# The last key tile of the second product in one stacked pass, ten odd rows in the correction, and x1's changed rows through DRAM

## The chip, the core and the metric
The kernel runs on one core of a Trainium2 chip. The metric is the device time of one execution in microseconds: before the change 171.88 us, the median of 3 runs (171.23 to 172.01). TensorE (PE) does matmuls, VectorE (DVE) elementwise work and reductions, ScalarE (ACT) scaling and roots, GpSimd (POOL) the gathers, SyncE (SP) most of the DMAs.

## The reference
Two graph layers over 1354 nodes of 512 features. The first is an attention over edges; the second a product with the adjacency and a weight.

```python
def layernorm(x): m, v = mean(x), var(x); return (x - m) / sqrt(v + 1e-5)

def L0(x, adj, pairs, Wq, bq, Wk, bk):          # 10000 pairs, 8 heads of 64
    sub, obj = pairs[:, 0], pairs[:, 1]
    att = sum over a head of (x[sub] @ Wq.T + bq) * (x[obj] @ Wk.T + bk) / 8
    scores = zeros(8, n, n);  scores[:, sub, obj] = att
    scores[no edge in adj] = -inf;  scores[diagonal] = 1e-7
    return softmax(scores, axis=2).sum(heads) / 8 @ x

x1  = layernorm(x + L0(x, adj, ...))
out = layernorm(x1 + adj @ (x1 @ W1) + b1)
```

## The kernel before
Nearly all scores are the same constant, since few of the given pairs are edges of the adjacency. So x1 is computed first for every row as if there were none (`sum_neighbours`, L1246: adjacency times x), and the rows with a real pair, at most 64 slots, are computed apart and put in as a correction. A count of pairs that doesn't fit sends every engine into a general path behind a branch (`overflow`, L270); with these inputs it isn't taken. Numbers are held as two f16 halves, high and low, so a product takes two or three matmuls.

Rows are in 11 tiles of 128, the last of 74. x1's tiles become ready one by one: ScalarE writes `x_sb` (L691) and the high half `x1s` (L694), VectorE the low half (L907). Then comes the first product of the second layer, x1 transposed times the adjacency (`mix_rows`, L1303 to L1316): 12 units (4 feature blocks by column spans of 512, 512 and 330), each accumulated over the 11 key tiles in two matmuls, one a half. `MIX_ORDER` sets their order: the first two units go side by side over all key tiles as x1 arrives, then unit by unit; the numbers in `mix_rows(a, b)` are positions in it. Each finished unit is split again into halves (`mix_high` on ScalarE, `mix_low` on VectorE).

Between pieces of that product TensorE does the small matmuls of the slots, in an order written out by hand: flags and numbering of the found pairs (L1320), transposes of gathered rows, queries and keys (L1352), scores (L1369), shares (L1375), the transposed change of x1 (L1380), and its product with W1 (L1387). GpSimd finds the candidates (L606, L611) and gathers x's rows, the sums and the adjacency's columns of the slots (L616 to L636); VectorE does the small steps between. `q` holds a slot's true row of x1, `kk` the row as first computed, `dx1` their difference where the slot counts (`rep`).

In the output stage each tile is 12 matmuls of the product's halves with W1's (`weigh`, L1397) and two of the correction (`correct`, L1421). The correction's stationary side `stackL` has 128 rows: 0 to 62 hold the slots' adjacency columns, 63 ones for the bias, 64 to 127 a one where a slot's row is the output row itself. Its moving side `stackR` holds in the same rows the change times W1, the bias, and `dx1`, as a high and a low half, hence two matmuls. VectorE adds `x_sb` (L1191) and takes moments, ScalarE normalises, SP stores. Six banks rotate (`OUTS`). SP's queue issues its DMAs in program order and stands still at a wait.

Of the kernel before, what the change touches and what calls it, by code (L numbers as in the profile page):

```python
# [34 lines left out]
BIAS_ROW = SLOTS - 1  # L35
SPANS = [(0, 512), (512, 1024), (1024, N)]
# [19 lines left out]
def resnorm_graph(nc, x, adj, pairs, pairs_left, b_qk, w1, b1, adj_t, adj_cols, wq_t, wk_t, adj_diag, out):  # L56
# [5 lines left out]
    with ExitStack() as ctx:  # L62
# [8 lines left out]
        sums_dram = nc.dram_tensor("sums_dram", [NP, GW], f32, kind="Internal").ap()  # L71
        live_map = nc.dram_tensor("live_map", [N, N], f32, kind="Internal").ap()
# [11 lines left out]
        col_rows = flat_stage[0:BIAS_ROW, KF * H:KF * H + N]  # L84
# [21 lines left out]
        stackR = sb("stackR", [P, 2, H], f16)  # L106
# [85 lines left out]
        dT = onehot[:, 0:2 * KF * SLOTS].rearrange("p (a n) -> p a n", a=2)  # L192
# [193 lines left out]
        def general_dve(dve):  # L386
# [186 lines left out]
        def _(pool):  # L573
# [49 lines left out]
            for b in range(YS):  # L623
# [8 lines left out]
                in_offset=bass.IndirectOffsetOnAxis(ap=slot_i[0:BIAS_ROW, 0:1], axis=0)).then_inc(cols_in, 16)  # L632
# [3 lines left out]
            nc.gpsimd.tensor_copy(stackL[0:BIAS_ROW, 0:N], col_rows).then_inc(cols_laid, 1)  # L636
            pool.wait_ge(cols_laid, 1)
# [5 lines left out]
        def _(act):  # L643
# [68 lines left out]
            nc.scalar.activation(stackL[0:64, :], col_no[0:64, :], ACT.Identity, bias=ones[0:64, 0:1], scale=0.0).then_inc(ones_laid, 1)  # L712
# [29 lines left out]
            nc.scalar.mul(dT[:, 0, :], tr[0][:, 0:KF * SLOTS], XS).then_inc(dT_hi, 1)  # L742
            act.wait_ge(change_ready, 1)
# [21 lines left out]
        def _(dve):  # L765
# [272 lines left out]
            step(V.tensor_scalar(fits, total[:], float(SLOTS), None, ALU.is_le))  # L1038
            dve.wait_ge(late_consts, 4)
# [3 lines left out]
            V.tensor_scalar(head_of[:, 1:2], row_no[:, 0:1], float(DK), None, ALU.is_ge)  # L1043
# [434 lines left out]
```

## Time and profile before

| what | us |
|---|---|
| timed runs, median | 171.88 |
| span of the profiled execution | 217.5 |
| TensorE matmuls busy | 166.0 (76%) |
| VectorE busy | 125.9 (58%) |
| ScalarE busy | 75.2 (35%) |
| GpSimd busy | 65.9 (30%) |

The profile is one execution. The page gives its span, 217.5 us, and no other time of its own; it is 45.6 us longer than the median of the timed runs. Times in the rows below are from the span's start. Matmuls overlap, so a busy TensorE is not one at its peak, and the mean ns of a matmul is longer than its step in a stream. Of the chain that ended last, 64% is TensorE and 22% "issue", time in which an engine waited for nothing shown.

### The profile page before, as it was taken

The page shows a single profiled execution, that of the slowest core. Times are in us where ns is not written, and L with a number is a line of the kernel's source. Part 1 is how long each engine was busy: PE and PEld are TensorE (multiplying, and loading weights), DVE is VectorE, ACT ScalarE, POOL GpSimd, SP SyncE. Part 2 cuts the span into 40 slices and gives each one's busy share as a digit, 9 for nine tenths or more (in the row PEclk, how much of TensorE's full clock was granted, in tenths as well). Part 3 has the DMA queues.
Part 4 walks back from the last instruction along what each step waited for, and adds up shares of the span by engine and source line. Part 5 has one row for each costly group of instructions (what it writes and reads, how often), then busy time and mean ns, then how long its engine had stood idle before and what let it go on. Part 6 is the DMA issues. An engine that isn't in the chain of part 4 may idle for free.

```text
span 217.5 us, 2923 instructions
## 1 busy us (share of the span) xinstructions
PE 166.0 (76%) x1053; PEld 84.6 (39%) x1053; DVE 125.9 (58%) x389; ACT 75.2 (35%) x126; POOL 65.9 (30%) x80
## 2 busy tenths in 40 slices
PE   4999521100011899999999999999999998999990
PEld 4844100000000245554454444475446553444450
DVE  3865360000400487887998967796989321766572
ACT  6677061000110177533237516261421120323333
POOL 7777777777771000000006723340000000000000
PEclk9999955555555599999999999999999999999998
DMA  6999959000000075189102200600000000122114
GB/s 184 387 352 308 327 178 357 29 0 0 1 0 0 15 217 184 48 278 371 45 37 77 22 0 18 190 5 6 0 0 0 3 2 9 50 99 96 51 73 145
DMA packets 12999, 22.65 MB, mean 104 GB/s; under 512 B 4478, under 2 KB 5662, under 8 KB 12850
## 3 DMA queue, kind: packets, MB, share of 16 engines
q1 hardware_dynamic: 7570, 18.17, 24.5%
q10 hardware_dynamic: 3280, 3.07, 4.1%
q0 software_dynamic: 2128, 1.16, 2.3%
q8 instruction: 10, 0.16, 0.3%
q14 instruction: 11, 0.09, 0.1%
HBM read 16.70 MB, written 5.68 MB: 103 GB/s over the span
## 4 chain that ended last, share of the span: by engine, by line
PE 64%; issue 22%; DVE 6%; POOL 4%; DMA 2%; ACT 0%; DVEq 0%; POOLq 0%
PE acc L1313 17%; PE acc L1246 15%; PE acc L1397 10%; PE tr L1246 7%; POOL found L611 3%; PE tr L1227 3%; PE tr L1232 3%; PE tr L1397 2%; DMA found<-in_adj,top_i 2%; PE acc L1421 2%; PE tr L1352 1%; PE tr L1387 1%; DVE st L845 1%; DVE y L894 1%; DVE hot L864 1%
## 5 line engine op out<-in xcount | busy, mean ns | idle before, releaser
L1313 PE MATMUL acc<-adjT,x1s 128*128 128x512 f16 (+3 forms) x264 | 52.4, 354 | 0.0
L606 POOL DMA_INDIRECT ed_adj<-in_adj,ed_idx x47 | 46.5, 989 | 14.5 <-issue 14.0
L1246 PE MATMUL acc<-xs,adjT 128*128 128x512 f16 (+1 forms) x176 | 43.1, 393 | 7.2 <-issue 7.1
L1313 PEld LDWEIGHTS acc<-adjT,x1s 128*128 128x128 f16 (+1 forms) x264 | 25.0, 98 | 23.4 <-issue 0.6
L1246 PEld LDWEIGHTS acc<-xs,adjT 128*128 128x128 f16 (+1 forms) x176 | 16.8, 99 | 30.9 <-issue 13.9
L1232 PE MATMUL tr<-bit_eye,adjT 128*128 128x65 f16 x121 | 7.4, 196 | 26.9 <-issue 26.9
L611 POOL DMA_INDIRECT found<-in_adj,top_i x8 | 8.7, 1084 | 50.9 <-DVE top_i L927 48.8
L1397 PE MATMUL acc<-whl,xs 128*128 128x512 f16 (+1 forms) x108 | 23.8, 370 | 0.0
L1246 PE MATMUL tr<-xs,adjT 128*128 128x512 f16 (+1 forms) x66 | 16.8, 388 | 7.3 <-issue 7.3
L1232 PEld LDWEIGHTS tr<-bit_eye,adjT 128*128 128x128 f16 x121 | 5.7, 98 | 30.0 <-issue 26.3
L825 DVE COPY counts<-tr 128x1 f32<-128x1 f32 x11 | 1.5, 140 | 26.9 <-remote 26.9
L658 ACT ACTIVATE st<-st,co 128x1 f32<-128x1 f32 x11 | 3.2, 293 | 37.9 <-DVE st L846 30.6
L1397 PEld LDWEIGHTS acc<-whl,xs 128*128 128x128 f16 x108 | 10.6, 98 | 11.8
L691 ACT ACTIVATE x_sb<-y,st 128x512 f32<-128x512 f32 x6 | 4.9, 810 | 27.4 <-issue 25.6
L699 ACT ACTIVATE xs<-acc 128x512 f16<-128x512 f32 (+1 forms) x12 | 6.4, 540 | 19.6 <-PE acc L1313 16.9
L647 ACT CAST adjT<-stage 128x1408 f16<-128x1408 f32 x9 | 12.2, 1363 | 1.3 <-DMA stage<-in_adj_T 0.5
L1246 PEld LDWEIGHTS tr<-xs,adjT 128*128 128x128 f16 (+1 forms) x66 | 6.3, 98 | 14.9 <-issue 8.2
L1191 DVE SCALAR_TENSOR_TENSOR y<-acc,x_sb 128x512 f32<-128x512 f32 x5 | 3.5, 692 | 10.1 <-PE acc L1421 10.1
L818 DVE SCALAR_TENSOR_TENSOR xs<-x_sb,xs 128x512 f16<-128x512 f32 x11 | 7.0, 684 | 3.4 <-ACT xs L663 1.9
L894 DVE SCALAR_TENSOR_TENSOR xd<-tr,co,x_sb 128x512 f32<-128x512 f32 x1 | 0.8, 751 | 13.8 <-remote 13.8
L845 DVE BATCH_NORM_STATS2 st<-y 128x6 f32<-128x512 f32 x12 | 8.3, 694 | 0.4
L1227 PE MATMUL tr<-ones 128*128 128x128 f16 x72 | 6.2, 272 | 2.8 <-POOL row_no L587 2.8
(273 smaller groups left out, 232.6 us busy)
## 6 DMA issues: line engine op xcount, KB each, us to landing
stage<-in_adj_T SPq DMA_DIRECT2D x9, 704.0 KB
x_sb<-in_x SPq DMA_DIRECT2D x3, 768.0 KB, 7.3
sums_dram<-y ACTq DMA_DIRECT2D x6, 256.0 KB
sums_dram<-xd ACTq DMA_DIRECT2D x5, 256.0 KB, 3.1
out<-y SPq DMA_DIRECT2D x5, 256.0 KB, 2.0
stage<-in_adj_T SPq DMA_DIRECT2D x3, 384.0 KB, 3.7
hot<-row_dram SPq DMA_DIRECT2D x1, 1024.0 KB
stage<-in_L_gnn_weight SPq DMA_DIRECT2D x1, 1024.0 KB, 5.3
```

Source lines behind the costliest of these rows:

```text
L606: nc.gpsimd.indirect_dma_start(out=ed_adj[0:EP, c:c + 1], out_offset=None, in_=adj_flat, in_offset=bass.IndirectOffsetOnAxis(ap=ed_idx[0:E ...
L611: nc.gpsimd.indirect_dma_start(out=found[0:EP, c:c + 1], out_offset=None, in_=adj_flat, in_offset=bass.IndirectOffsetOnAxis(ap=top_i[0:EP, ...
L647: nc.scalar.copy(adjT[:, :, t * P:(t + 1) * P], stage[:, t % RING, :].rearrange("p (k i) -> p k i", k=T)).then_inc(adj_cast, 1)
L691: nc.scalar.activation(x_sb[:, i, :], y4(i), ACT.Identity, bias=st[:, i % 2, 9:10], scale=st[:, i % 2, 8:9]).then_inc(x1_ready, 1)
L699: nc.scalar.mul(mix[:, 0, u % KF, i:j], mix_bank(u)[:, 0:j - i], 1.0 / XS).then_inc(mix_hi, 1)
L818: V.scalar_tensor_tensor(xs[:, 1, t, :], x_sb[:, t, :], XS, xs[:, 0, t, :], ALU.mult, ALU.subtract).then_inc(x_lo, 1)
L845: step(V.bn_stats(s[:, 0:6], v))
L1227: mm(tr[2][:, 0:P], ones16[:], ones16[:], start=True, stop=True)
L1232: last = mm(tr[t % 2][:, 0:WP + 1], adjT[:, k, t * P:(t + 1) * P], bit_eye[:, k, :], start=(k == 0), stop=(k == T - 1))
L1246: last = mm(sum_bank(i)[:, :], adjT[0:width[k], k, i * P:(i + 1) * P], xs[0:width[k], half, k, :], start=(k == 0 and half == 0), stop=(k = ...
L1313: ins = mm(mix_bank(u)[:, 0:j - i], x1s[0:width[k], half, k, f * P:(f + 1) * P], adjT[0:width[k], k, i:j], start=(k == 0 and half == 0), s ...
L1397: last = mm(bank, mix[:, a, k, t * P:(t + 1) * P], whl[:, b, k, columns], start=(k == 0 and m == 0), stop=False)
```

## The change
The last key tile's 74 rows are cut in 64 and 10. For the 64, `x1_tail` holds the high half in partitions 0 to 63 and the low half in 64 to 127, and `adj_tail` the adjacency rows twice, so one matmul does both halves. SP lays both by DMA from `x1s` and `adjT`. The ten odd rows go into the correction: their adjacency rows into `stackL` and their x1 into `dx1`'s rows 53 to 62, so slots hold at most 53 pairs (`CAP`).

The correction no longer adds the change itself to x1. SP stores each x1 tile to DRAM (`x1_dram`), GpSimd scatters the true rows `q` over it by index (`back_i`), and SP loads x1 back into `x_sb` in four parts; VectorE waits for them in the output stage. That frees the lower 64 rows of the correction, which now hold the low half of the upper ones, so it is one matmul a tile. The change's product with W1 (L1387) is made for 128 rows, the slots twice, and GpSimd's column gather and cast too.

```diff
+EVEN = 64
+ODD = LAST - EVEN
+CAP = BIAS_ROW - ODD
+BACK_PARTS = ((0, 1), (1, 5), (T - 1, T), (5, T - 1))
+BACK_BEFORE = {0: 0, 1: 1, 5: 2, 6: 3}
...
# SP
+            for half in range(2):
+                sp.dma_start(adj_tail[EVEN * half:EVEN * half + EVEN, 0:N], adjT[0:EVEN, T - 1, 0:N]).then_inc(tail_laid, 16)
+            for t in range(T):
+                sp.wait_ge(x1_ready, t + 1)
+                sp.dma_start(rows(x1_dram, t), x_sb[0:width[t], t, :]).then_inc(x1_stored, 16)
+            sp.wait_ge(x1_hi, T)
+            sp.dma_start(x1_tail[0:EVEN, :], x1s[0:EVEN, 0, T - 1, :]).then_inc(tail_laid, 16)
+            sp.wait_ge(x1_lo, T)
+            sp.dma_start(x1_tail[EVEN:P, :], x1s[0:EVEN, 1, T - 1, :]).then_inc(tail_laid, 16)
+            sp.wait_ge(odd_zeroed, 1)
+            sp.dma_start(x1_odd[CAP:BIAS_ROW, :], x_sb[EVEN:LAST, T - 1, :]).then_inc(odd_in, 16)
+            sp.wait_ge(ones_laid, 1)
+            for half in range(2):
+                sp.dma_start(stackL[SLOTS * half + CAP:SLOTS * half + BIAS_ROW, 0:N], adjT[EVEN:LAST, T - 1, 0:N]).then_inc(odd_laid, 16)
             sp.wait_ge(bias_split, 2)
-            sp.dma_start(stackR[BIAS_ROW:BIAS_ROW + 1, :, :], bias_hl[:, :, :]).then_inc(biased, 16)
+            for half in range(2):
+                at = SLOTS * half + BIAS_ROW
+                sp.dma_start(stackR[at:at + 1, :], bias_hl[:, half, :]).then_inc(biased, 16)
+            sp.wait_ge(x1_scattered, 16)
+            for n, (a, b) in enumerate(BACK_PARTS):
...
+                    sp.dma_start(x_sb[:, a:b, :], x1_dram[a * P:b * P, :].rearrange("(t p) h -> p t h", p=P)).then_inc(x1_back[n], 16)
# GpSimd
+            pool.wait_ge(adj_cast, T - 2)
+            nc.gpsimd.memset(x1_odd, 0.0).then_inc(odd_zeroed, 1)
             pool.wait_ge(top_ready, 1)
...
-                in_offset=bass.IndirectOffsetOnAxis(ap=slot_i[0:BIAS_ROW, 0:1], axis=0)).then_inc(cols_in, 16)
+                in_offset=bass.IndirectOffsetOnAxis(ap=slot_i[:, 0:1], axis=0)).then_inc(cols_in, 16)
...
-            nc.gpsimd.tensor_copy(stackL[0:BIAS_ROW, 0:N], col_rows).then_inc(cols_laid, 1)
+            nc.gpsimd.tensor_copy(stackL[0:CAP, 0:N], col_rows[0:CAP]).then_inc(cols_laid, 1)
+            nc.gpsimd.tensor_copy(stackL[SLOTS:SLOTS + CAP, 0:N], col_rows[SLOTS:SLOTS + CAP]).then_inc(cols_laid, 1)
+            pool.wait_ge(back_ready, 1)
+            pool.wait_ge(row_ready, 1)
+            pool.wait_ge(x1_stored, 16 * T)
+            nc.gpsimd.indirect_dma_start(
+                out=x1_dram, out_offset=bass.IndirectOffsetOnAxis(ap=back_i[:, 0:1], axis=0),
+                in_=q[0:SLOTS, :], in_offset=None, bounds_check=N - 1, oob_is_err=False).then_inc(x1_scattered, 16)
# ScalarE
-            nc.scalar.mul(dT[:, 0, :], tr[0][:, 0:KF * SLOTS], XS).then_inc(dT_hi, 1)
+            nc.scalar.mul(dT[:, 0], twice(tr[0]), XS).then_inc(dT_hi, 1)
-            nc.scalar.mul(stackR[64:P, 0, :], dx1[64:P, :], WS).then_inc(right_hi, 1)
-            nc.scalar.mul(stackR[0:BIAS_ROW, 0, :], tr[2][0:BIAS_ROW, :], 1.0 / XS).then_inc(right_hi, 1)
+            for at in (SLOTS, 0):
+                nc.scalar.mul(stackR[at:at + BIAS_ROW, :], tr[2][at:at + BIAS_ROW, :], 1.0 / XS).then_inc(right_hi, 1)
# VectorE
-            V.tensor_scalar(stackL[64:P, :], col_no[64:P, :], sub[64:P], None, ALU.is_equal).then_inc(low_ready, 1)
+            step(V.tensor_scalar(slot[0:SLOTS, 10:11], rep[0:SLOTS], -FAR, FAR, ALU.mult, ALU.add))
+            V.tensor_tensor(back_i[:, :], slot[0:SLOTS, 10:11], slot[0:SLOTS, 0:1], ALU.add).then_inc(back_ready, 1)
...
+            dve.wait_ge(odd_in, 16)
+            step(V.tensor_scalar(x1_odd, x1_odd, fits[0:SLOTS], None, ALU.mult))
...
-            step(V.tensor_tensor(dx1, q, kk, ALU.subtract))
-            V.tensor_scalar(dx1, dx1, rep, None, ALU.mult).then_inc(change_ready, 1)
+            step(V.tensor_tensor(dx1[0:SLOTS], q[0:SLOTS], kk[0:SLOTS], ALU.subtract))
+            V.scalar_tensor_tensor(dx1[0:SLOTS], dx1[0:SLOTS], rep[0:SLOTS], x1_odd, ALU.mult, ALU.add).then_inc(change_ready, 1)
...
-            V.scalar_tensor_tensor(dT[:, 1, :], tr[0][:, 0:KF * SLOTS], XS, dT[:, 0, :], ALU.mult, ALU.subtract).then_inc(dT_lo, 1)
+            for two in range(2):
+                V.scalar_tensor_tensor(dT[:, 1, :, two], tr[0][:, 0:KF * SLOTS].rearrange("p (k s) -> p k s", k=KF), XS, dT[:, 0, :, two],
+                                       ALU.mult, ALU.subtract).then_inc(dT_lo, 1)
...
+                if t in BACK_BEFORE:
+                    dve.wait_ge(x1_back[BACK_BEFORE[t]], 16)
# TensorE
-                    for half in range(2):
-                        ins = mm(mix_bank(u)[:, 0:j - i], x1s[0:width[k], half, k, f * P:(f + 1) * P], adjT[0:width[k], k, i:j], ...)
+                    if k < T - 1:
+                        ...
+                    else:
+                        pe.wait_ge(tail_laid, 16 * 4)
+                        mm(mix_bank(u)[:, 0:j - i], x1_tail[:, f * P:(f + 1) * P], adj_tail[:, i:j],
+                           start=False, stop=True).then_inc(mix_done, 1)
...
-                for half in range(2):
-                    last = mm(bank, stackL[:, t * P:(t + 1) * P], stackR[:, half, columns], start=False, stop=(half == 1))
-                last.then_inc(out_done, 1)
+                mm(bank, stackL[:, t * P:(t + 1) * P], stackR[:, columns], start=False, stop=True).then_inc(out_done, 1)
```

How the instructions stand. TensorE, in the first product where the tail of its first two units and the flags come; `x1s` and `adjT` are the operands of full tiles, `adj_tail` and `stage` those of the stacked tail. Before:
```order
L1313 MATMUL acc<-adjT,x1s 128x512 x3
L1313 MATMUL acc<-adjT,x1s 128x512 [waits x1_lo]
L1313 MATMUL acc<-adjT,x1s 128x512 x3
L1313 MATMUL acc<-adjT,x1s 128x512 [waits y_ready]
L1313 MATMUL acc<-adjT,x1s 128x512 x17
L1320 MATMUL acc<-flag,below 128x8 [waits flags_ready]
L1321 MATMUL acc<-flag,ones 128x8
L1313 MATMUL acc<-adjT,x1s 128x512 x4
```
Now:
```order
L1371 MATMUL acc<-adjT,x1s 128x512 x3
L1375 MATMUL acc<-adj_tail,stage 128x512 [waits tail_laid,x1_lo]
L1375 MATMUL acc<-adj_tail,stage 128x512 [waits tail_laid]
L1371 MATMUL acc<-adjT,x1s 128x512 [waits y_ready]
L1371 MATMUL acc<-adjT,x1s 128x512 x17
L1380 MATMUL acc<-flag,below 128x8 [waits flags_ready]
L1381 MATMUL acc<-flag,ones 128x8
L1371 MATMUL acc<-adjT,x1s 128x512 x2
L1375 MATMUL acc<-adj_tail,stage 128x512 [waits tail_laid]
L1371 MATMUL acc<-adjT,x1s 128x512 [waits y_ready]
```
The four tail matmuls of the two units have become two, which wait for the tail's DMAs, and the next unit's two one.

SP, from the last weight load to the bias row (before, the bias row stood right behind the load). Before:
```order
L553 DMA stage<-in_L_gnn_weight 128x4x512 [waits adj_cast]
L554 DMA wT<-in_L_gnn_Wq_T 128x4x512
L555 DMA wT<-in_L_gnn_Wk_T 128x4x512
L557 DMA stackR<-wraw 1x16x64 [waits bias_split]
L273 TENSOR_LOAD count_i [waits count_ready]
```
Now (`x_dram` is x1 in DRAM, the first `stage` rows the tail, the last the ten odd rows):
```order
L575 DMA wT<-in_L_gnn_Wk_T 128x4x512
L577 DMA adj_tail<-adjT 64x1354 x2
L580 DMA x_dram<-x_sb 128x512 [waits x1_ready] x10
L580 DMA x_dram<-x_sb 74x512 [waits x1_ready]
L582 DMA stage<-x1s 64x512 [waits x1_hi]
L584 DMA stage<-x1s 64x512 [waits x1_lo]
L586 DMA stage<-x_sb 10x512 [waits odd_zeroed]
L589 DMA stackL<-adjT 10x1354 [waits ones_laid]
L589 DMA stackL<-adjT 10x1354
L593 DMA stackR<-wraw 1x16x32 [waits bias_split]
L593 DMA stackR<-wraw 1x16x32
L597 DMA x_sb<-x_dram 128x512 [waits x1_scattered]
```
Eighteen DMAs that wait for x1's tiles or come behind them stand ahead of the bias row, and behind it the reload waits for the scatter.

TensorE, at the start of the output stage (`whl` and `xs` are `weigh`, `stackR` and `stackL` the correction). Before:
```order
L1421 MATMUL acc<-stackR,stackL 128x512 [waits right_lo,right_hi,biased,low_ready,cols_laid]
L1421 MATMUL acc<-stackR,stackL 128x512
L1421 MATMUL tr<-stackR,stackL 128x512 x2
L1397 MATMUL acc<-whl,xs 128x512 [waits mix_lo]
L1397 MATMUL acc<-whl,xs 128x512 x11
L1421 MATMUL acc<-stackR,stackL 128x512 x2
```
Now:
```order
L1480 MATMUL acc<-stackR,stackL 128x512 [waits right_lo,right_hi,biased,odd_laid,cols_laid]
L1480 MATMUL tr<-stackR,stackL 128x512
L1457 MATMUL acc<-whl,xs 128x512 [waits mix_lo]
L1457 MATMUL acc<-whl,xs 128x512 x11
L1480 MATMUL acc<-stackR,stackL 128x512
```
Each correction is one matmul; the first waits for the odd rows in place of the compare.

## Rows read from the trace of the kernel before
**Rows 1.** The page's slices: TensorE's granted clock, in tenths of full speed.
```profile
PEclk9999955555555599999999999999999999999998
```

**Rows 2.** Windows: length; PE, PEld, DVE, ACT, POOL busy (count); clock, DMA share, GB/s.
```profile
27.00:72.00 45.00, 6.09 (x18) 1.94 (x19) 5.74 (x19) 5.88 (x8) 30.15 (x32) 0.51 0.21 70
```

**Rows 3.** Chain of waits in time: start us, us, engine and tile, line, count.
```profile
152.13 8.74 PE acc L1313 x40
...
161.44 8.23 PE acc L1313 x58
...
184.38 2.59 PE acc L1397 x12
...
186.97 0.43 PE acc L1421 x2
```

**Rows 4.** TensorE's waits from 105 us to the end: us in total, times, longest.
```profile
PE acc L1421 <- issue: 1.0, 1, 1.0
PE acc L1320 <- DVE flag L943: 0.3, 1, 0.3
```

**Rows 5.** Groups by shape, 110 to 183 us: operation, shape, count, busy us, mean ns.
```profile
L1313 PE MATMUL acc<-adjT,x1s 128*128 128x512 f16 x160 | 36.9, 379 | 0.0
...
L1313 PE MATMUL acc<-adjT,x1s 74*128 74x512 f16 x16 | 4.6, 379 | 0.0
...
L1313 PE MATMUL acc<-adjT,x1s 74*128 74x330 f16 x8 | 1.8, 304 | 0.0
```

**Rows 6.** Timeline, VectorE, output stage: start, us, operation, idle before it.
```profile
196.50 0.69 DVE L1191 SCALAR_TENSOR_TENSOR y<-acc,x_sb 128x512 f32<-128x512 f32 x1 [1.09 <-PE acc L1421]
```

**Rows 7.** Chain of waits at the flags.
```profile
124.91 4.28 DMA found<-in_adj,top_i
...
129.90 0.18 PE acc L1320
```

**Rows 8.** Timeline: the first product's start, and x1's tile 10.
```profile
116.06 2.11 PE L1313 MATMUL acc<-adjT,x1s 128*128 128x512 f16 x9
...
118.89 0.81 ACT L691 ACTIVATE x_sb<-xd,st 128x512 f32<-128x512 f32 x1 [0.60 <-DVE st L851]
```

**Rows 9.** The 74-row output store: its issue, and two windows behind it.
```profile
202.33 0.29 SPq L562 DMA_DIRECT2D out<-y  x1
...
203.00:204.00 1.00, 1.00 (x6) 0.48 (x5) 0.93 (x3) 0.00 (x0) 0.00 (x0) 1.00 0.14 37
...
207.00:208.00 1.00, 1.00 (x7) 0.43 (x5) 0.44 (x3) 0.47 (x1) 0.00 (x0) 1.00 0.07 27
```

**Rows 10.** Timeline of GpSimd and VectorE at the cast, and one at 171 us.
```profile
141.65 2.28 DVE L1067 SCALAR_TENSOR_TENSOR whl<-stage,whl 128x2048 f16<-128x2048 f32 x1
...
142.65 2.45 POOL L636 CAST stackL<-stage 63x1354 f16<-63x1354 f32 x1 [4.10 <-DMA stage<-in_adj_cols,slot_i]
...
143.85 1.79 DVE L1069 SCALAR_TENSOR_TENSOR xo<-wraw,xo 64x512 f16<-64x512 f32 x1
...
171.16 0.69 DVE L1174 SCALAR_TENSOR_TENSOR stackR<-wraw,stackR 64x512 f16<-64x512 f32 x1 [0.23 <-ACT stackR L744]
```

**Rows 11.** Timeline: the weight load of the shares' matmul.
```profile
160.72 0.10 PEld L1375 LDWEIGHTS tr<-xo,wraw 128*128 128x128 f16 x1 [0.34 <-DVE wraw L1148]
```

**Rows 12.** Timeline: last step of the change, and its transposed form.
```profile
168.33 0.49 DVE L1168 TENSOR_SCALAR wraw<-wraw 128x512 f32<-128x512 f32 x1
...
170.09 0.38 ACT L742 ACTIVATE onehot<-tr 128x256 f16<-128x256 f32 x1 [1.90 <-PE tr L1380]
...
170.51 0.42 DVE L1172 SCALAR_TENSOR_TENSOR onehot<-tr,onehot 128x256 f16<-128x256 f32 x1 [0.87 <-ACT onehot L742]
```

**Rows 13.** The replaced rows, the last weight load's landing, the first output tile.
```profile
167.03 0.55 DVE L1166 TENSOR_SCALAR wraw<-wraw,st 128x512 f32<-128x512 f32 x1
...
wT<-in_L_gnn_Wk_T SPq DMA_DIRECT2D x1, 1024.0 KB, 11.4
...
183.98 0.69 DVE L1191 SCALAR_TENSOR_TENSOR y<-acc,x_sb 128x512 f32<-128x512 f32 x1 [5.78 <-PE acc L1421]
```

More of the change, by code:

```diff
@@ L105, in resnorm_graph @@
         table = sb("table", [P, P], f16)
-        stackR = sb("stackR", [P, 2, H], f16)
+        stackR = sb("stackR", [P, H], f16)
+        adj_tail = sb("adj_tail", [P, NP], f16)
+        free = KF * H + N
+        x1_odd = flat_stage[0:SLOTS, free:free + H]
+        x1_tail = flat_stage[:, free + H:free + H + H // 2].bitcast(f16)
+        back_i = sb("back_i", [SLOTS, 1], i32)
         ident = sb("ident", [P, P])
@@ L190, in resnorm_graph @@
         bias_hl = raw[0:1, 3 * KF * H - H:3 * KF * H].bitcast(f16).rearrange("p (a h) -> p a h", a=2)
-        dT = onehot[:, 0:2 * KF * SLOTS].rearrange("p (a n) -> p a n", a=2)
+        dT = onehot[:, :].rearrange("p (a k two s) -> p a k two s", a=2, k=KF, two=2)
         mix = xs[:, :, :, :].rearrange("p a t h -> p (a t h)").rearrange("p (a k i) -> p a k i", a=2, k=KF)
@@ L402, in general_dve @@
                 dve.wait_ge(y_stored[b], 16 * len(range(b, T, YS)))
+            for part in x1_back:
+                dve.wait_ge(part, 16)
             step(V.tensor_scalar(pos_all, ed_ok[0:EP], -float(N * N), float(N * N), ALU.mult, ALU.add))
@@ L509, in y4, with twice @@
             return (y if t % 4 < 2 else xd)[:, t % 2, :]
+        def twice(bank):
+            return bank[:, 0:KF * SLOTS].rearrange("p (k s) -> p k s", k=KF).unsqueeze(2).broadcast_to([P, KF, 2, SLOTS])
         def edge_slice(n):
@@ L711, in _ @@
             act.wait_ge(late_consts, 4)
-            nc.scalar.activation(stackL[0:64, :], col_no[0:64, :], ACT.Identity, bias=ones[0:64, 0:1], scale=0.0).then_inc(ones_laid, 1)
+            nc.scalar.activation(stackL[:, :], col_no[:, :], ACT.Identity, bias=ones[:, 0:1], scale=0.0).then_inc(ones_laid, 1)
             mix_high(3)
@@ L1037, in _ @@
             V.tensor_scalar(count_i[:], total[:], float(E), None, ALU.min).then_inc(count_ready, 1)
-            step(V.tensor_scalar(fits, total[:], float(SLOTS), None, ALU.is_le))
-            dve.wait_ge(late_consts, 4)
-            V.tensor_scalar(stackL[64:P, :], col_no[64:P, :], sub[64:P], None, ALU.is_equal).then_inc(low_ready, 1)
+            step(V.tensor_scalar(fits, total[:], float(CAP), None, ALU.is_le))
             mix_low(2)
@@ L1071, in _ @@
             dve.wait_ge(keys_ready, 1)
-            dve.wait_ge(biased, 16)
+            dve.wait_ge(biased, 16 * 2)
             for k in range(KF):
@@ L1165, in _ @@
             step(scale_shift(norm_b))
-            step(V.tensor_scalar(q, q, norm_b[:, 8:9], norm_b[:, 9:10], ALU.mult, ALU.add))
-            step(V.tensor_tensor(dx1, q, kk, ALU.subtract))
-            V.tensor_scalar(dx1, dx1, rep, None, ALU.mult).then_inc(change_ready, 1)
+            V.tensor_scalar(q, q, norm_b[:, 8:9], norm_b[:, 9:10], ALU.mult, ALU.add).then_inc(row_ready, 1)
+            dve.wait_ge(row_ready, 1)
+            step(V.tensor_tensor(dx1[0:SLOTS], q[0:SLOTS], kk[0:SLOTS], ALU.subtract))
+            V.scalar_tensor_tensor(dx1[0:SLOTS], dx1[0:SLOTS], rep[0:SLOTS], x1_odd, ALU.mult, ALU.add).then_inc(change_ready, 1)
             mix_low(8)
@@ L1311, in mix_rows @@
                         pe.wait_ge(x1_lo, k + 1)
-                    for half in range(2):
-                        ins = mm(mix_bank(u)[:, 0:j - i], x1s[0:width[k], half, k, f * P:(f + 1) * P], adjT[0:width[k], k, i:j],
-                                 start=(k == 0 and half == 0), stop=(k == T - 1 and half == 1))
-                    if k == T - 1:
-                        ins.then_inc(mix_done, 1)
+                    if k < T - 1:
+                        for half in range(2):
+                            mm(mix_bank(u)[:, 0:j - i], x1s[:, half, k, f * P:(f + 1) * P], adjT[:, k, i:j],
+                               start=(k == 0 and half == 0), stop=False)
+                    else:
+                        pe.wait_ge(tail_laid, 16 * 4)
+                        mm(mix_bank(u)[:, 0:j - i], x1_tail[:, f * P:(f + 1) * P], adj_tail[:, i:j],
+                           start=False, stop=True).then_inc(mix_done, 1)
             mix_rows(0, 31)
@@ L1382, in _ @@
             mix_rows(117, 122)
-            pe.wait_ge(dT_lo, 1)
+            pe.wait_ge(dT_lo, 2)
             pe.wait_ge(w1_lo, 1)
@@ L1386, in _ @@
                 for n, (a, b) in enumerate(((0, 0), (0, 1), (1, 0))):
-                    last = mm(tr[2][0:64, :], dT[:, a, k * SLOTS:(k + 1) * SLOTS], whl[:, b, k, :],
+                    last = mm(tr[2][:, :], dT[:, a, k].rearrange("p two s -> p (two s)"), whl[:, b, k, :],
                               start=(k == 0 and n == 0), stop=(k == KF - 1 and n == 2))
```

31 lines of the change are left out of this document (18 added, 13 removed).

## The prediction
> **What bounds the kernel now.** I read the page's slices first, then the windows, the chain of waits, and last the waits of TensorE alone. The profiled span is 217.5 us and the timed median 171.88. The slices and windows show why: from 27 to 72 us TensorE gets through 18 matmuls in 45 us, at a granted clock near 0.5, one in 2.5 us, with nothing shown that it waits for [rows 1, 2]. At the pace found elsewhere 18 matmuls take under 4 us; the rest, over 41 of the 45.6 us between span and median, is this pause, which I take to be absent from the timed runs. The page gives the profiled execution no time beside its span, so differences are worked out on the span and carried to 171.88 unscaled. All that the change touches lies behind the pause, at full clock.
>
> From 130 us to the end the chain of waits is nearly all TensorE: first product (L1313) 40 matmuls in 8.74 us, that is 0.2185 us for one of 512 columns; 58 in 8.23 us, 0.142 for one of 330; the output stage alternates 12 matmuls in 2.59 us and a correction pair in 0.43 [rows 3]. In the whole stretch from 105 us TensorE's own list has two entries: 1.0 us before the first correction, which is the branch on the count, and 0.3 us for the flags [rows 4]. So a matmul less is time less, except just ahead of a point where TensorE meets a chain of another engine with no room.
>
> **What is removed.** The last key tile has 74 rows, yet its matmuls last as long as those of 128: mean 379 against 379 ns at 512 columns [rows 5]. The 16 of 512 columns and 8 of 330 become 8 and 4. 8 x 0.2185 + 4 x 0.142 = 2.32 us. The 24 corrections become 12: ten tiles and the two parts of the last (320 and 192 columns, one tile together) at 0.43 / 2 = 0.215 each, 11 x 0.215 = 2.37 us. Together 4.69 us. In the output stage all of it counts: VectorE waits 1.09 us for TensorE in every tile [rows 6], so a tile 0.215 shorter still leaves it the faster engine. Ahead of that stage five points give something back.
>
> **Flags.** The first two stacked passes stand before the wait for the flags. That wait ends with GpSimd's lookups and a landing at 129.2, then three VectorE steps; TensorE's first matmul behind it starts at 129.90 [rows 7]. None of this moves, so two passes, 0.44 us, are lost.
>
> **The tail's arrival.** The stacked operands come by DMA, on SP's queue, behind the store of x1's tile 10 (74 rows, 148 KB). Before, the matmuls start at 116.06 and the 41st, the first on the tail, would start at 116.06 + 40 x 0.216 (2.59 / 12) = 124.7 [rows 3, 8]. Tile 10 of x1 is written at 118.89 + 0.81 = 119.7 [rows 8]. The trace has one transfer of the very shape of the new store, the output store of 74 rows, issued at 202.33: in the microsecond from 203 the queues move 37 GB/s at a DMA share of 0.14, and in that from 207, with the next, full store gone by in between, still 27 at 0.07 [rows 9]. So about two of 16 engines carry it, for some 5.6 us from issue. Issued at 119.75, it ends at 125.35; two small transfers behind it on the same engines, 0.3 us, make 125.65. TensorE then has 20 passes to the flags, 4.37 us, and is there at 130.0 instead of 129.9: 0.1 us. Bounds: nothing (the tail overtakes the store), or one for one with each microsecond beyond.
>
> **Query and key part.** GpSimd's one cast of 63 rows becomes two of 53, with the same 1354 columns each, and the gather ahead of them brings 128 rows instead of 63. The trace has the cast at 142.65 for 2.45 us; a VectorE operation on two SBUF inputs that starts at 143.85 lasts 1.79 us, where the same shape elsewhere takes 0.69 [rows 10]. It ends 0.54 us behind the cast. I read this as the cast starting in earnest when the 2048-column operation ends (143.93), running 1.17 us, and VectorE waiting for it. Two casts of 1.17 us with VectorE's 0.54 between them are over by 147; the query-key products behind them then reach TensorE about when it is through the ten matmuls it does meanwhile. I take 0.2 us; bounds 0 and 2.45 - 0.5 (a full second cast ahead of the chain). The Trainium skill, page SBUF — State Buffer, section Who interferes with whom, says that a VectorE instruction with two SBUF inputs and a GpSimd instruction that reads SBUF exclude each other, and that the first to start holds the port for its whole length. By that rule, the trace agrees (1.79 against 0.69 us), and which of the two starts first is what decides; the sum would be the 0.2 us or the 1.2 us of the rival below.
>
> **Shares.** Two more stacked passes stand before the shares' matmul. TensorE's weight load there already waited 0.34 us on VectorE and starts at 160.72 [rows 11]; VectorE's chain sets that point. Of 0.44 us only some 0.1 can be had: 0.35 lost.
>
> **Change rows.** The last step to the change goes from a scale (0.49, ending at 168.8 [rows 12]) to a two-input add (0.69 [rows 10]): +0.2 us. Behind the 58 matmuls TensorE comes to it at 161.44 + 8.23 = 169.67 [rows 3]; two 330-column passes less leave some 0.4 us of room. Then the transposed change is written twice: ScalarE 0.38 becomes about 0.6 us (512 columns), VectorE one 0.42 becomes two [rows 12]. 0.6 + 2 x 0.42 + 0.1 of gaps = 1.55 us, against nine passes of cover, 9 x 0.142 = 1.28: 0.3 lost. The widened product keeps its 12 matmuls of 512 columns.
>
> **Scatter and reload.** The replaced rows are final at 167.03 + 0.55 = 167.6 [rows 13]. GpSimd's issue and the landing together took 4.3 us at the last lookup [rows 7]; the scatter is done at 172. SP then reloads 2.65 MB. Three loads of 1 MB landed 11.4 us after issue [rows 13], so by 183 or so all but the slow 74-row one; the first tile, 256 KB, allowed as long as that lookup's 4.3 us, is there at 176. VectorE needs it at 183.98 [rows 13], the next four tiles from 1.5 us later, the rest only five and more tiles of 3 us on. Cost nothing; the cover is 8 us, and six output banks give more. Behind SP's new wait stand the branch and the output stores, the first of them after the first tile is normalised, so they are not held up either. The stores of x1's full tiles go out behind the three weight loads, beside no adjacency load. Two single-column VectorE operations for the scatter index and one of 512 columns for the ten rows take the place of the compare over 64 rows and 1408 columns that goes: nothing net, at most a few tenths, which the range holds.
>
> **Sum.** 4.69 - 0.44 - 0.1 - 0.2 - 0.35 - 0.3 = 3.30 us. 171.88 - 3.3 = **168.6 us**; the span, with the same pause, 214.2.
>
> **The rivals.**
> *Everything arrives* (the tail overtakes, VectorE's chains start earlier with TensorE): 4.69 us, 167.2. For it: VectorE is itself released by TensorE at several places. Against it: the flags hang on GpSimd. 0.10.
> *Two casts in a row.* The larger gather lands later, both casts run together and hold VectorE up in the scores' chain, which TensorE meets with under 0.5 us of room. One cast more, 1.17 us: 168.6 + 1.2 = 169.8. For it: the 1.79 us of [rows 10]; against it: VectorE's operations around 145 us read PSUM and one SBUF operand. 0.14.
> *The tail comes late.* Each microsecond beyond 125.65 costs one. Place: the 41st matmul, where all of TensorE's later work queues. Gain and loss are even at 125.65 + 3.3 = 128.95; from 129.8 the kernel is slower by over 0.5%. If the 74-row store, now beside other stores, takes 10.3 us where it took 5.6, the tail lands at 119.75 + 10.3 + 0.3 = 130.35: 168.6 + 4.7 = 173.3 us. If 8.9 us, 128.95: no change, 171.9. For it: that store has only a few engines and all later SP transfers stand behind it; against it: the queues are nearly empty then. 0.09 for a slower kernel, 0.09 for no change.
> *The reload comes late.* It would have to be over 8 us late to be felt; its chance is in the width of the others. That the change doesn't do what it says is excluded for the matmul counts; that a pass of 128 rows costs more than one of 74 is excluded by [rows 5].
>
> **How the numbers follow.** Forecast 0.58, with its own range 167.7 to 169.6. Faster by over 0.5% (0.86 us, about what a measurement tells): 0.58 + 0.10 + 0.14 = 0.82; within it 0.09; slower 0.09. The range reaches down past the full 4.69 us with some noise, 166.9, and up over the cast at its far bound, 168.6 + 1.95 = 170.5, and part of the late tail: 171.3.
>
> **What would show it.** 12 tail matmuls and 12 corrections; about 2.81 us from tile to tile at the end, where it was 3.02. A wait of about 1 us of TensorE before the 41st matmul of the first product, none over 0.3 at the flags. A wait of some 0.7 us at the shares, 0.3 before the widened product. No VectorE wait on reloaded x1. I am wrong if TensorE waits over 2 us for the tail, if the scores' matmul waits on VectorE by a microsecond, or if the output stage is paced by VectorE or the reload.

## The result, and the profile after

| | before | after |
|---|---|---|
| median | 171.67 us (20 runs, 170.58 to 172.75) | 171.02 us (20 runs, 169.27 to 173.85) |
| ratio | | 0.9925, 95% interval 0.9898 to 0.9951 |
| profiled execution | span 217.5 us, with the pause | 169.27 us, span 167.5, no pause |

The change is worth 0.7 to 1.3 us (by medians and by the ratio), where 3.3 us were forecast. All ratios here leave out the executions that took over 1.5% longer than the fastest of the same kernel, and the medians keep them. The pause of [rows 1, 2] is gone; the 51 executions of before that were timed beside the experiments have spans of 169.0 to 173.1 us, so it was indeed no part of the timed runs. The 20 of after spread over 4.6 us, those of before over 2.2, and the profiled execution of after is the fastest of its 20.

The profile after; of its slices the one of TensorE's granted clock, which answers to [rows 1]:
```profile
PEclk9999999999999999999999999999999999999997
```
The matmuls of the first product by shape, 68 to 136 us, which answer to [rows 5] (count, busy us, mean ns, idle before):
```profile
L1371 PE MATMUL acc<-adjT,x1s 128*128 128x512 f16 x160 | 36.7, 379 | 0.0
...
L1375 PE MATMUL acc<-adj_tail,stage 128*128 128x512 f16 x8 | 2.9, 378 | 1.4 <-DMA stage<-x1s 1.4
L1375 PE MATMUL acc<-adj_tail,stage 128*128 128x330 f16 x4 | 1.2, 303 | 0.0
```
Eight and four stand where 16 and 8 of 74 rows were, at the same time for each: the removal is what it was said to be. TensorE's list of waits ("issue" is time in which it waited for nothing that the profile shows), which answers to [rows 4] (us in total, times, longest):
```profile
PE acc L1480 <- issue: 1.6, 1, 1.6
PE acc L1375 <- DMA stage<-x1s: 1.4, 1, 1.4
PE tr L1435 <- DVE wraw L1202: 0.3, 1, 0.3
```
The 1.0 us at the branch has become 1.6, and there is a wait for the tail. Both are in the chain of waits (start us, us), which answers to [rows 3, 7]:
```profile
73.79 4.59 DMA stage<-x1s
78.51 0.59 PE acc L1375 x2
79.11 3.88 PE acc L1371 x18
83.02 0.45 PE acc L1371 x2
...
131.31 2.59 PE tr L1457 x12
133.90 1.62 issue
135.52 0.38 PE acc L1480
```
Laid over each other at the start of the first product (116.06 before, 68.32 after), TensorE's steps stand so, after less before: flags +0.67 us, the product of the query and key part 0, scores -0.21, shares -0.37, first of the widened product -0.53, first weight product -0.72, first correction -0.09, VectorE's start on the last tile of the chain -2.25. So 0.6 us is lost ahead of the flags, 1.39 are won behind them up to the first weight product, 0.63 is lost again at the branch, and the output stage wins 10 x 0.215 in full.

### The profile page after: what moved, and what is told of

It reads as the page before. It is cut to its first block, busy times and chain, and to the rows that moved or that the text cites. A ratio compares the mean times of both kernels' runs of the same rounds, so it can differ in the third digit from the quotient of the medians.

```text
span 167.5 us, 2910 instructions
## 1 busy us (share of the span) xinstructions
PE 155.2 (93%) x1029; PEld 82.1 (49%) x1029; DVE 124.7 (74%) x391; ACT 75.2 (45%) x126; POOL 68.1 (41%) x83
## 4 chain that ended last, share of the span: by engine, by line
PE 73%; DVE 15%; issue 4%; DMA 3%; ACT 2%; POOL 1%; DVEq 0%; POOLq 0%
PE acc L1371 17%; PE acc L1303 17%; PE acc L1457 12%; PE tr L1303 9%; PE tr L1284 4%; PE tr L1457 3%; DMA stage<-x1s 3%; PE tr L1289 2%; DVE st L896 2%; PE tr L1412 2%; PE tr L1447 2%; DVE x1s L958 1%; PE acc L1480 1%; PE acc L1375 1%; DVE y L945 1%
## 5 line engine op out<-in xcount | busy, mean ns | idle before, releaser
L1371 PE MATMUL acc<-adjT,x1s 128*128 128x512 f16 (+1 forms) x240 | 48.9, 354 | 0.0
L1303 PE MATMUL acc<-xs,adjT 128*128 128x512 f16 (+1 forms) x176 | 40.1, 379 | 0.0
L1371 PEld LDWEIGHTS acc<-adjT,x1s 128*128 128x128 f16 x240 | 22.8, 98 | 20.9 <-issue 0.2
L1303 PE MATMUL tr<-xs,adjT 128*128 128x512 f16 (+1 forms) x66 | 15.2, 379 | 0.0
L686 POOL DMA_INDIRECT x_dram<-wraw,back_i x1 | 1.3, 1342 | 21.0 <-DVE wraw L1220 21.0
L710 ACT ACTIVATE st<-st,eps 128x1 f32<-128x1 f32 x13 | 3.7, 284 | 13.6 <-DVE st L897 13.6
L1284 PE MATMUL tr<-ones 128*128 128x128 f16 x72 | 7.0, 293 | 2.8 <-POOL row_no L629 2.8
L921 DVE SCALAR_TENSOR_TENSOR xs<-acc,xs 128x512 f16<-128x512 f32 (+1 forms) x12 | 7.3, 619 | 2.6 <-ACT xs L751 2.6
L808 ACT ACTIVATE y<-y,st 128x512 f32<-128x512 f32 x6 | 4.9, 813 | 8.6 <-DVE st L902 8.6
L1284 PEld LDWEIGHTS tr<-ones 128*128 128x128 f16 x72 | 6.9, 140 | 2.8 <-POOL row_no L629 2.8
```

The costliest lines, as they stand in the source:

```text
L710: return nc.scalar.activation(s[:, 10:11], s[:, 7:8], ACT.Sqrt, bias=floor)
L921: V.scalar_tensor_tensor(mix[:, 1, u % KF, i:j], mix_bank(u)[:, 0:j - i], 1.0 / XS, mix[:, 0, u % KF, i:j], ALU.mult, ALU.subtract).then_i ...
L1284: mm(tr[2][:, 0:P], ones16[:], ones16[:], start=True, stop=True)
L1303: last = mm(sum_bank(i)[:, :], adjT[0:width[k], k, i * P:(i + 1) * P], xs[0:width[k], half, k, :], start=(k == 0 and half == 0), stop=(k = ...
L1371: mm(mix_bank(u)[:, 0:j - i], x1s[:, half, k, f * P:(f + 1) * P], adjT[:, k, i:j], start=(k == 0 and half == 0), stop=False)
```

## The experiments

Each was timed in turn with the kernel before. e0 to e3 were timed together on one chip (before: 171.73 median), e4 to e7 on another (172.37), f0 to f3 on a third (171.84); what is compared across them is the ratio to before. In the traces of these kernels line numbers shift by some lines; the waits named "issue" ahead of the first correction are the branch, those for `stage<-x1s` the tail. The theory: the 4.69 us of matmuls are gone, and two transfers cost time that the forecast gave them nothing or 0.1 for: the copy of the tail arrives late, and the reload is in flight when TensorE takes its branch. The rivals: the traffic costs by its volume, wherever it lies; or the loss lies in the added work of VectorE and GpSimd.

**The changed kernel again (e0).** No edit.


> The changed kernel once more, beside the others. Both theories expect a median 0.5 to 1.2 us below the kernel before, with runs spread over 4 us. Theory A (the idle TensorE of 1.5 us in front of the stacked tail is what both costs time and lets the granted clock fall in some executions): the longer executions show a mean clock of 0.981 to 0.987, the shorter ones 0.99 and more. Rival B (the fall belongs to the 1.6 us of idle at the branch before the first correction, beside the reload): the same numbers here, it differs in the next two kernels. Rival C (the stores of x1 beside the first layer delay that layer).


171.71 us (170.24 to 175.25, 12 runs), ratio 0.9964 (0.992 to 1.0008). In its profiled execution the branch took 1.9 us and the tail 1.6. The interval of the ratio takes in 1, so these 12 executions alone don't show a gain.

**The tail's copies first (e1).**
```
+ the two x1_tail DMAs
  the store of x1's tile 10 (was ahead of them)
```


> SP issues the two transfers of the tail's halves ahead of the store of x1's tile 10; nothing else differs from the changed kernel. Theory A: the tail lands about 2 us after its issue at 73.8, so TensorE waits under 0.2 us at the 41st matmul instead of 1.4, the flags' matmul comes 0.6 us earlier (TensorE is then held by the flags themselves), and the executions with a low clock go: median 1.2 to 2.5 us below the changed kernel's, 168.5 to 169.8. Rival B: 0.6 us off each execution, the spread and the low clocks stay, median about 170.4. Rival C: as B.


169.87 us (169.6 to 172.77, 6 runs), ratio 0.9893 (0.985 to 0.9937). The wait went to 0.22 us as expected, but the copies land nearly 4 us after their issue and not about 2. Copy and first matmul on the tail in e1's timeline (start, us; in brackets the idle time ahead and what ended it):
```profile
74.37 0.47 SPq L584 DMA_DIRECT2D stage<-x1s  x1
...
78.18 0.59 PE L1376 MATMUL acc<-adj_tail,stage 128*128 128x512 f16 x2 [0.22 <-DMA stage<-x1s]
```
From the second copy's issue to the matmul it is 3.81 us here and 3.95 in the profiles of e4 and f2, which share this edit; in the five with the store ahead it is 4.7 to 6.0 (after 4.72, e0 5.16, f1 4.82, f0 5.72, e2 6.02). In e5, without any store, TensorE reaches the tail 3.42 us after that issue and does not wait.

**No reload (e2).** Scatter and reload left out, stores kept; the changed rows of x1 then lack their change in the output.
```
- indirect DMA of the changed rows, the four reload DMAs, VectorE's waits on them
```


> The changed kernel without the scatter of the true rows and without the reload of x1, so the output lacks x1's change itself; the stores of x1 stay. Theory A: TensorE's gap before the first correction falls from 1.6 to 1.0 us, 0.6 us off every execution, and the executions with a low clock stay: median about 170.4. Rival B: the low clocks go, median about 168.9. Rival C: nothing but the 0.6 us at most.


169.93 us (169.31 to 173.77, 6 runs), ratio 0.9894 (0.9843 to 0.9946). The wait at the branch is back at 0.9 us, while the tail came later than in any other profile:
```profile
PE acc L1359 <- DMA stage<-x1s: 2.7, 1, 2.7
PE acc L1464 <- issue: 0.9, 1, 0.9
```

**The traffic alone (e3).** The kernel before, with x1's stores, scatter and reload added; the changed rows get their change twice.
```
+ store of each x1 tile; two VectorE steps for the index; scatter; four reload DMAs; VectorE's waits on them
```


> The kernel before with the stores of x1, the scatter and the reload added, and nothing taken away (x1's change is added twice in the output). It prices the new traffic by itself. Theory A: 0.6 us slower than before (the branch gap 1.0 becomes 1.6), no low clocks: ratio 1.002 to 1.005. Rival B: 0.6 us and low clocks in some executions, median up 1.5 to 2.5 us. Rival C: 1 to 2 us slower with TensorE's first layer stretched.


175.35 us (174.42 to 176.62, 6 runs), ratio 1.0209 (1.0156 to 1.0263): 3.6 us, where 0.6 was expected. The chain of waits and the windows (length; PE, PEld, DVE, ACT, POOL busy; clock, DMA share, GB/s) show where:
```profile
132.89 2.59 PE tr L1426 x12
135.48 2.37 issue
137.85 0.59 PE acc L1450 x2
138.44 0.43 PE tr L1450 x2
138.87 4.28 PE acc L1426 x12
143.15 0.43 PE acc L1450 x2
143.58 2.59 PE acc L1426 x12
```
```profile
125.00:135.00 10.00, 10.00 (x55) 5.19 (x53) 1.59 (x3) 1.37 (x3) 0.00 (x0) 1.00 0.89 258
135.00:138.00 3.00, 0.63 (x4) 0.13 (x2) 0.00 (x0) 0.00 (x0) 0.00 (x0) 1.00 0.23 76
...
140.00:141.00 1.00, 1.00 (x4) 0.30 (x2) 0.96 (x3) 0.29 (x1) 0.00 (x0) 0.50 0.00 0
```
The branch takes 2.4 us instead of 1.0, behind ten microseconds in which the reload had the DMA engines 0.89 busy. Then the granted clock is 0.50, that is the lower level of 1.2 GHz, for some 3.4 us in all: the next twelve matmuls take 4.28 us instead of 2.59. 1.4 + 1.7, and about 0.5 more at the flags (a wait of 0.8 us, not 0.3), make the 3.6 in this execution.

**Tail first, and the reload's last two parts held (e4).**
```
  (as e1)
  for n, (a, b) in enumerate(BACK_PARTS):
+     if n == 2:
+         sp.wait_ge(early_read, 1)
```
`early_read` is raised by the last weight product ahead of the branch (of two output tiles; the expectation's six is a slip), so 1,428 KB start only then.


> The changed kernel with the stacked tile's two copies ahead of the last x1 store (as in the second experiment), and the last two of the four reload transfers (1,428 KB) held until TensorE has ended the six early tiles' weight products, that is until it stands at its branch on the count. Nothing else changes. Theory A, the branch's target instructions are fetched through the same DMA engines that carry the reload: the gap of TensorE at the branch falls from 1.9 us (second experiment's profile) to the 0.9 to 1.1 us of the kernels that have no reload there, the granted clock stays at 1.00 after it, the median is 168.6 to 169.3 us (0.983 to 0.987 of before), and the runs spread less. The held rows land by about 142 us, ahead of the output tile that adds them (about 150 us), so nothing waits for them. Rival B, the reload costs by its volume wherever it lies (memory, ports): gap 1.6 to 1.9 us, or time lost elsewhere, median 169.9 as before.


168.62 us (168.35 to 170.13, 6 runs), ratio 0.9815 (0.9765 to 0.9866). Its waits, and two windows:
```profile
PE acc L1483 <- issue: 0.9, 1, 0.9
PE acc L1378 <- DMA stage<-x1s: 0.6, 1, 0.6
PE acc L1383 <- DVE flag L997: 0.4, 1, 0.4
```
```profile
134.00:136.00 2.00, 1.39 (x7) 0.71 (x8) 0.94 (x2) 0.00 (x0) 0.00 (x0) 1.00 0.24 42
136.00:138.00 2.00, 2.00 (x11) 0.89 (x10) 1.91 (x4) 0.29 (x1) 0.00 (x0) 1.00 1.01 289
```
The same bytes now move at a DMA share of 1.01 beside a TensorE that is busy throughout, and cost no time; VectorE never waits on them. It does wait 1.2 us once for an output store to finish, which it did not in the profile of after; TensorE sets the pace there, so this cost nothing either. Ahead of the branch the reload's first two parts still fill the engines, but only until 129 us, 4.7 us before the gap begins.

**No traffic (e5).** Stacked tail and single correction alone, no stores, scatter or reload; the changed rows lack their change in the output.


> The changed kernel without the ten x1 stores, the scatter of the changed rows and the reload; x1's changed rows then lack their change in the final sum. What is left is the stacked tile and the single correction product. Theory A: this is the ceiling of the change: before's 171.7 less 4.69 us of matmuls, plus what VectorE, ScalarE and the copies still give back (0.3 at the shares, 0.3 at the change rows, 0.2 at the tail and flags): 167.3 to 168.2 us, 0.975 to 0.980, branch gap 0.9 to 1.0, tail wait under 1.2. Rival B, the traffic costs nothing and the loss lies in the added VectorE and GpSimd work: 169.5 to 170, as the runs without reload.


168.20 us (167.91 to 170.97, 7 runs), ratio 0.9767 (0.9726 to 0.9808): 4.0 us. Its profiled execution was the longest of the seven, 170.97: VectorE had the flags at 83.8 us, where it had them at 82.3 in after and 82.6 in e4, TensorE waited 2.0 us for them, and the clock fell behind that wait (windows as above):
```profile
PE acc L1360 <- DVE flag L976: 2.0, 1, 2.0
```
```profile
82.00:84.00 2.00, 0.13 (x3) 0.13 (x4) 0.71 (x5) 0.00 (x0) 0.00 (x0) 1.00 0.01 0
84.00:86.00 2.00, 2.00 (x9) 0.74 (x8) 1.76 (x11) 1.22 (x2) 0.00 (x0) 0.71 0.00 0
86.00:88.00 2.00, 2.00 (x10) 0.88 (x8) 0.54 (x4) 2.00 (x2) 0.00 (x0) 0.50 0.00 0
```
The change's added work of VectorE and GpSimd, but for the scatter, is in this kernel, so the rival that puts the loss there (169.5 to 170) is out.

**The traffic alone, held (e6).** e3 with the same hold as in e4; again the changed rows get their change twice.


> The kernel before with x1's stores, the scatter and the reload added (as in the fourth experiment, in which it took 175.35), but with the reload's last two transfers held until TensorE stands at its branch. x1's changed rows get their change twice, as there. Theory A: the gap at the branch falls from 2.4 to about 1.0 us, and since TensorE is not idle for as long, the granted clock stays at 1.00 where it was 0.50 for 3.6 us: 1.4 and 1.7 us come back, 172.0 to 172.6. Rival B, volume: 175 again. Rival C, only the gap comes back and the clock falls for another reason: 173.9.


172.36 us (171.24 to 175.3, 12 runs), ratio 1.0007 (0.9976 to 1.0038). Of TensorE's waits in its profile:
```profile
PE acc L1452 <- issue: 0.9, 1, 0.9
```
The whole 3.6 us of e3 is gone and not a byte is saved. This rules out the rival of volume. e3 with e6 settles that the loss lies in when the reload runs, and the profiles put it at the branch.

**One correction alone (e7).** The kernel before, one of its two correction products left out (the output lacks the low-order halves).
```
- for half in range(2): mm(bank, stackL, stackR[:, half])
+ mm(bank, stackL, stackR[:, 0])
```


> The kernel before with one of the two correction products per output tile left out (the low-order halves of the differences are then missing from the result): the second part of the change alone, without stores, scatter, reload or stacked tile. Theory A: 11 times 0.215 us come off in full, because TensorE paces the output stage: 2.2 to 2.4 us, 169.3 to 169.5, ratio 0.986 to 0.987. Rival: VectorE takes the pace over and half or more of it stays: over 0.993.


169.24 us (168.88 to 171.73, 4 runs), ratio 0.9826 (0.9756 to 0.9895). That is 3.0 us by the ratio, with an interval of 1.8 to 4.2, so the 2.37 us are there; part of the rest may be the branch, 0.5 us in this profile. With e5 this leaves about 1.0 us (0.9826 less 0.9767) for the stacked tail, of whose 2.32 the forecast left 0.93 behind its deductions; the intervals of the two overlap, so that split is rough.

**Both costs side by side (f0 to f3).** f0 is the changed kernel, f1 has only the hold of e4, f2 both edits (e4 again), f3 both edits and also this:
```
  the two x1_tail DMAs
+ the store of x1's tile 9 (was ahead of them)
  the store of x1's tile 10
```


> The changed kernel as it is, beside the three other kernels of this job, so that each edit is told apart on one chip. 170.9 to 171.8 us, 0.992 to 0.997 of before, in two groups: about 170.3 where the gap at the branch stays under 2 us, 172 to 174 where it doesn't and the granted clock falls after it.

> The changed kernel with the reload's last two transfers held until TensorE stands at its branch, and nothing else. Theory A (two independent costs: the gap at the branch 0.7 to 0.9 us and now and then the clock after it; the tail's late arrival 0.2 to 1.0 us ahead of the flags): 169.0 to 169.8, branch gap 0.9, tail wait 1.4 to 2. Rival, the tail's late arrival is the larger cost: 170.5 or more.

> The changed kernel with both edits, as in the fifth experiment, again beside the control. Theory A: 168.4 to 169.0, 0.980 to 0.984 of before, no run much over 170.

> Both edits, and the store of x1's tile 9 also behind the stacked tile's two copies, so that nothing of 256 KB is in flight ahead of them. Theory A: the wait of 0.6 us before the tail's first matmul goes to under 0.2, but the flags' matmul then waits longer for GpSimd's gathers and VectorE (0.4 to 1.0 us), since these, and not the tail, set when the flags are ready: 168.3 to 168.8, same as with both edits. Rival, the tail still sets it: 167.8 or less.

| | median, range (runs) | ratio to before (95%) | branch, tail in the profile |
|---|---|---|---|
| f0 | 171.22, 169.58 to 174.53 (13) | 0.9936 (0.9898 to 0.9973) | 2.4, 2.1 us |
| f1, hold | 169.79, 168.65 to 171.81 (6) | 0.9867 (0.9815 to 0.9919) | 0.4, 1.6 |
| f2, both | 169.45, 168.65 to 170.51 (6) | 0.9845 (0.9795 to 0.9895) | 1.0, 1.0 |
| f3 | 169.17, 168.44 to 169.51 (6) | 0.9829 (0.9788 to 0.987) | 0.6, 1.9 |

The hold gives 1.4 us by the medians; the intervals of f0 and f1 just overlap, and it is e3 against e6 that stands clear of the noise. The tail's order gave 1.8 us from e0 to e1 and 0.3 on top of the hold here (f1 to f2); the intervals overlap both times, so its size stays open between nothing and some 2 us. f2 and f3 came out some 0.4 us above what was expected of them, and f0's executions lie spread and not in two groups. The expectation for f3's tail was wrong: its wait did not go under 0.2, and in its timeline the landing is as late as with a store ahead:
```profile
73.94 0.47 SPq L584 DMA_DIRECT2D stage<-x1s  x1
...
79.15 0.59 PE L1379 MATMUL acc<-adj_tail,stage 128*128 128x512 f16 x2 [1.88 <-DMA stage<-x1s]
```
That is 5.2 us from the copy's issue, with two stores issued 0.5 and 1.1 us behind it. What is behind the copies counts too, then, or the landing varies by a microsecond for another cause; one profile can't say which. The median is about that of both edits, as the theory had it.

f0's profiled execution took 174.53 us, the longest of its 13, and shows how the long runs come about:
```profile
PE acc L1480 <- issue: 2.4, 1, 2.4
PE acc L1375 <- DMA stage<-x1s: 2.1, 1, 2.1
```
```profile
80.00:82.00 2.00, 0.69 (x4) 0.36 (x5) 0.57 (x2) 0.28 (x1) 0.52 (x1) 1.00 0.05 11
82.00:84.00 2.00, 2.00 (x7) 0.76 (x6) 1.49 (x4) 0.81 (x2) 0.00 (x0) 0.57 0.02 1
84.00:86.00 2.00, 2.00 (x6) 0.71 (x5) 1.21 (x10) 0.00 (x0) 0.00 (x0) 0.58 0.00 0
```
Both waits are longer by 0.7 to 0.8 us than in the profile of after, the clock fell behind the one for the tail, and the first layer was late as well: TensorE waits 1.9 us in all for ScalarE's casts between 20 and 49 us, before the first store of x1.

The version with both edits beats both kernels: 0.9815 (e4) and 0.9845 (f2) of before, and 0.9829 for f3, against 0.9925, 0.9964 and 0.9936 for the change as it was.

The timed runs have no trace, but each has its mean granted clock. One fall as in f0 takes 0.010 off it (3.4 us at half of 173). It is 0.987 or less in 15 of the 45 executions of the changed kernel (after, e0, f0), whose median is 173.1 us against 170.6 for the other 30; in 1 of before's 51; and in 1 of the 18 with both edits (e4, f2, f3). So about a third of the changed kernel's executions are some 2.5 us longer at a lower clock, and with both edits that is rare. The bound is rough: e3's profiled execution has a fall at a mean of 0.988.

## Why the prediction was wrong, step by step

**Removed, 4.69 us: right.** 12 matmuls and 12 corrections, 2.81 us from tile to tile (136.11, 138.92, 141.72 in the chain of after). Only ten of the eleven 0.215 us count, since the chain leaves TensorE for VectorE ahead of the last tile. The kernel without traffic gains 4.0 us by the ratio.

**Flags and the tail's arrival, 0.44 + 0.1: too small.** The landing was forecast for 125.65, that is 77.9 in after's time; it came at 78.5, and TensorE's 20 passes from there reach the flags at 82.83. VectorE had them sooner:
```profile
82.14 0.17 DVE L994 TENSOR_SCALAR flag<-top_key 128x8 f16<-128x8 f32 x1
...
82.83 0.17 PE L1380 MATMUL acc<-flag,below 128*128 128x8 f16 x1
```
Where TensorE stands waiting (e1, e4, f2, f3), its matmul starts 0.06 us behind VectorE's end. So of the 0.67 us lost at the flags 0.46 is the late tail, where 0.1 was forecast, and 0.21 the flags themselves, which the forecast had not moving. Against each profile's own flags the late tail costs 0.3 us in e0, 0.4 in f1, 1.2 in e2 and 2.7 in f0, of which 1.7 is the clock that fell. The mechanism was the forecast's (one for one beyond the bound); the landing was sized on one case, the 74-row output store, and its spread was not in the forecast's own range but in the rival of the late tail. That rival's store of 10 us never came: the latest landing was 6.0 us after the copy's issue, in e2.

**Query and key part, 0.2: nothing was lost.** Three passes fewer between the flags and this product are 0.66 us, and TensorE's steps went from +0.67 to 0. The rival of two casts in a row did not happen. The VectorE operation of [rows 10] that had lasted 1.79 us lasted 0.68, since it now began 0.22 us ahead of the cast, which then took 1.63 us, 1.17 of them behind VectorE's end (start, us). This agrees with the rule weighed in the prediction (the Trainium skill, SBUF — State Buffer, Who interferes with whom), that the first to start holds the port.
```profile
96.34 0.68 DVE L1123 SCALAR_TENSOR_TENSOR xo<-wraw,xo 64x512 f16<-64x512 f32 x1
```
```profile
96.56 1.63 POOL L680 CAST stackL<-stage 53x1354 f16<-53x1354 f32 x1 [5.34 <-DMA stage<-in_adj_cols,slot_i]
98.25 1.31 POOL L681 CAST stackL<-stage 53x1354 f16<-53x1354 f32 x1
```

**Shares and change rows, 0.35 + 0.3: near.** The two weight loads of TensorE that wait for VectorE there:
```profile
112.77 0.10 PEld L1435 LDWEIGHTS tr<-xo,wraw 128*128 128x128 f16 x1 [0.77 <-DVE wraw L1202]
...
123.29 0.76 PEld L1447 LDWEIGHTS tr<-whl,onehot 128*128 128x128 f16 x5 [0.45 <-DVE onehot L1228]
```
0.77 against some 0.7, and 0.45 against 0.3. From the flags to the first weight product 1.39 us were won (from +0.67 to -0.72), where 1.88 in passes less 0.85 left 1.03: 0.36 more than forecast, 0.2 of it at the queries and keys.

**Scatter and reload, nothing: this is the step that failed.** The forecast asked only when VectorE needs the rows: it never waits on them. It did not ask what else may depend on the DMA engines, which the reload fills from 125 to 133 us. TensorE comes to its branch right behind that, and the gap there is 1.6, 1.9, 1.9, 2.4 and 2.4 us in the five profiles in which the whole reload is issued at once, 0.4 to 1.0 in the nine in which there is none or its larger part is held.

How the reload reaches TensorE is argued and not shown. The Trainium skill, page Runtime: NRT & Kernel Launch, section Instruction fetch mechanics, says that a taken branch to a target outside the two pages held forces a DMA fetch of that page first. With these inputs the general path is passed over, so this would be the jump over its instructions. The traces agree as far as they go: the gap is long where the engines are full until under 1 us ahead of it, in f0 at a DMA share of 1.00 up to 138 us with the gap from 138.4. But within the gap the share is under 0.3 (0.11 in after from 134 to 135), so TensorE does not simply wait beside full engines, and no trace shows which packet it waited for, or whether it was one for the branch.

**The sum.** From the first product on 2.26 us were won between the two profiles, 1.04 fewer than forecast: 0.57 at the flags and 0.63 at the branch, less 0.16 elsewhere (0.36 more up to the first weight product, 0.2 fewer in the output stage). The median won still less: the profiled execution was the fastest of 20, both waits are longer in the profiles of e0 and f0, and a third of the executions have the lower clock, which the forecast gave no term. With both waits shortened the gain is 2.7 to 3.2 us by the ratios, next to the 3.3 of the forecast. That closeness is partly luck: in e4's profile 0.4 us fewer than forecast are won at the flags and 0.2 fewer in the output stage, and 0.45 more are won elsewhere.

## What to carry to other kernels

Ask of a bulk transfer not only when its data is needed, but what every engine does while it is in flight and just behind it; a branch is one such point. Held until TensorE stood at its branch, 1.4 MB cost nothing; issued early they cost 3.6 us (e3 against e6) and some 1.4 us in the changed kernel (f0 against f1). Small copies that an engine is about to need may be better off ahead of large stores in a queue: here it was worth between nothing and 2 us. A wait's length varies from run to run, and TensorE's clock can fall behind it: size it with its spread, not by one execution, and compare the runs' mean clocks with those of the kernel before.

## What the runs showed of the hardware

- TensorE's gap at its branch was 0.4 to 1.0 us with the DMA engines nearly free for 4 us ahead of it and 1.6 to 2.4 us with a reload that filled them until under 1 us ahead (14 profiles; e3 against e6 with the same bytes).
- TensorE's granted clock fell from 1.00 to 0.50 for about 3.4 us behind idle stretches of 2.4 us (e3, branch), 2.0 (e5, flags) and 2.1 (f0, tail). It did not behind the 2.7 us of e2's wait for the tail or the 2.4 us of f0's branch. So a wait of the same length may bring the fall or not. Each fall cost 1.7 us.
- Two copies of 64 KB landed 3.8 to 4.0 us after the second one's issue with one store behind them (e1, e4, f2), 4.7 to 6.0 us with a 148 KB store of 74 rows just ahead of them (five profiles), and 5.2 us with none ahead and two close behind (f3).
- A VectorE operation on two SBUF inputs took 1.79 us beside a GpSimd cast that had begun 1.2 us ahead of it (before), and 0.68 us where it began 0.22 us ahead of the cast (after).
